# Cross-attention and MoE kernel: fp32 hidden chunks and fp32 w2 in the down product, with no halves of either

## The reference

```python
x = x + xattn(layernorm(x), ctx, w_q, w_kv, w_out, b_out)   # 16 heads of 64, softmax over 77 keys
x = x + ffn(layernorm(x), router_w, w1, w2, w3, sw1, sw2, sw3)

# ffn, x2 = 8192 rows of 128; 8 experts of 176 hidden units; the 2 best experts of a row
logits = x2 @ router_w.T
gate = zeros(T, 8); gate[row, idx of its top 2] += logits
for e in range(8):
    h = silu(x2 @ w1[e].T) * (x2 @ w3[e].T)
    moe_out += gate[:, e:e+1] * (h @ w2[e].T)
sh = silu(x2 @ sw1.T) * (x2 @ sw3.T)                        # the shared expert, all rows
moe_out += sh @ sw2.T
```

## Time and profile before

| | us |
|---|---|
| median of 3 runs | 1155.31 |
| lowest and highest | 1151.79, 1160.76 |
| the profiled execution, its own time | 1144.55 |
| its span, first to last instruction | 1142.7 |
| mean granted TensorE clock | 0.931 |
| PE busy | 956.3 (84%) |
| DVE busy | 900.6 (79%) |
| POOL busy | 736.9 (64%) |
| ACT busy | 716.1 (63%) |

### The profile page before, as it was taken

The page is one execution under the profiler, slowest core; times in us unless marked ns, Lnnn a source line. Parts: engine busy times, 40 slices in busy tenths (PEclk is TensorE's granted clock), DMA queues, the critical chain, the costliest instruction groups (busy, mean ns, idle before and its releaser), DMA issues.

```text
span 1142.7 us, 30302 instructions
## 1 busy us (share of the span) xinstructions
PE 956.3 (84%) x10072; PEld 786.8 (69%) x10072; DVE 900.6 (79%) x2010; ACT 716.1 (63%) x1574; POOL 736.9 (64%) x1141
## 2 busy tenths in 40 slices
PE   5856889999999998889999999887466778888772
PEld 5555778887887876777788787666355667777441
DVE  4676688997997887778799788889436868888994
ACT  3544687777777775556677677654345648777651
POOL 3232467557788777556788787865666646565765
PEclk9879899999999999888999999988678989999996
DMA  8053232533344432222443444434333456566853
GB/s 263 6 180 43 35 61 55 138 61 58 73 74 62 71 71 57 49 49 53 99 73 69 66 72 62 71 76 102 66 93 109 127 142 166 161 165 161 163 143 115
DMA packets 222789, 107.45 MB, mean 94 GB/s; under 512 B 160464, under 2 KB 214384, under 8 KB 221456
## 3 DMA queue, kind: packets, MB, share of 16 engines
q1 hardware_dynamic: 214448, 88.47, 36.3%
q0 software_dynamic: 8192, 17.06, 5.2%
HBM read 39.15 MB, written 35.06 MB: 65 GB/s over the span
## 4 chain that ended last, share of the span: by engine, by line
PE 34%; DVE 18%; issue 15%; POOL 12%; ACT 9%; DMA 9%; SPq 1%; POOLq 0%; DVEq 0%; ACTq 0%
DMA OT_lo<-O_lo 6%; PE Q L1315 5%; PE S L1249 4%; DVE top L1007 3%; POOL O_lo L584 3%; PE W L1204 3%; PE W L1191 3%; DVE pt_lo L1048 2%; PE W L1205 2%; PE W L1206 2%; PE W L1193 2%; PE W L1192 2%; PE S L1302 2%; DVE P L1017 2%; POOL w_raw L609 2%
## 5 line engine op out<-in xcount | busy, mean ns | idle before, releaser
L1048 DVE TENSOR_TENSOR pt_lo<-Q,pt_hi 77x512 f16<-77x512 f32 x256 | 164.9, 680 | 101.0 <-ACT pt_hi L701 100.4
L609 POOL DMA_INDIRECT w_raw<-ys,pos_y x128 | 129.8, 1014 | 73.3 <-issue 37.9
L584 POOL TENSOR_TENSOR O_lo<-O,O_hi 128x512 f16<-128x512 f32 x128 | 147.8, 1175 | 38.2 <-ACT O_hi L709 24.1
L701 ACT ACTIVATE pt_hi<-Q 77x512 f16<-77x512 f32 x256 | 144.8, 590 | 41.5 <-PE Q L1315 40.7
L490 POOL DMA_INDIRECT xs<-x2cat,pos x128 | 133.0, 1039 | 43.0 <-issue 21.8
L1315 PE MATMUL Q<-ident,P 128*77 128x128 f32 x1024 | 155.8, 288 | 1.1 <-ACT P L684 0.7
L1302 PE MATMUL S<-v_hi,pt_hi 96*128 96x65 f16 x1024 | 118.7, 203 | 32.5 <-DVE P L1017 30.6
L1249 PE MATMUL S<-G,xTm 128*128 128x462 f32 (+1 forms) x384 | 144.9, 513 | 0.6 <-ACT G L691 0.6
L1302 PEld LDWEIGHTS S<-v_hi,pt_hi 96*128 96x128 f16 x1024 | 99.3, 101 | 47.5 <-DVE P L1017 38.5
L1315 PEld LDWEIGHTS Q<-ident,P 128*77 128x77 f32 x1024 | 128.9, 156 | 2.6 <-ACT P L684 1.2
L520 POOL TENSOR_TENSOR x2cat<-x2f,x2cat 128x128 f16<-128x128 f32 x64 | 27.3, 427 | 152.3 <-ACT x2cat L666 152.3
(11 more groups left out here) (280 smaller groups left out, 3273.8 us busy)
## 6 DMA issues: line engine op xcount, KB each, us to landing
ys<-ysb SPq DMA_DIRECT2D x44, 256.0 KB
xg_early<-xs SPq DMA_DIRECT2D x60, 132.0 KB
xp<-x2cat SPq DMA_DIRECT2D x64, 64.0 KB, 1.5
y_out<-X SPq DMA_DIRECT2D x16, 256.0 KB
xg_late<-xs SPq DMA_DIRECT2D x28, 132.0 KB
xs<-zero_in SPq DMA_DIRECT2D x3, 1056.0 KB, 10.8
xs<-zero_in SPq DMA_DIRECT2D x24, 132.0 KB, 2.6
X<-x_in SPq DMA_DIRECT2D x1, 2304.0 KB, 9.6
```

The lines of the kernel that those rows point to most:

```text
L584: pool.tensor_tensor(O_lo[:, half_], O[:, (t + 1) % 2, half_], O_hi[:, half_], ALU.subtract).then_inc(s["p_Olo"], 1)
L609: pool.indirect_dma_start(out=Yr[:, q % YR, k, i * D:(i + 1) * D], out_offset=None, in_=ys_d[batch_part(b)][:, :], in_offset=index(pos_y, ...
L701: act.activation(pt_hi[0:NK, j % 2, c * 512:(c + 1) * 512], QB[q_bank(j, c)][0:NK, :], ACT.Copy).then_inc(s["a_PThi"], 1)
L1048: dve.tensor_tensor(pt_lo[0:NK, j % 2, c * 512:(c + 1) * 512], QB[q_bank(j, c)][0:NK, :], pt_hi[0:NK, j % 2, c * 512:(c + 1) * 512], ALU.s ...
```

## The change

h is kept in fp32: DVE writes hC (now with the scale of w3, on all its 48 rows, straight from PSUM rows 64 to 111) and hA into rings of three, and nothing splits them. w2 is one fp32 tensor, scaled once by ACT. `down` is 2 fp32 matmuls per block of 128 rows, 8 per item in the place of 20. `hC_s`, `hA_hi`, `hA_lo`, `high`, `low`, `low_C`, `low_A` and `w2_lo` are gone. All results of routed items leave through ACT. Three orders differ as well: ACT's `O_high` comes before `turn_out` in a slot and no longer after the last `pt_high`; PE's `turn` comes after the ups of an item and no longer before them; `project(65)` comes after `up_B(0)`. `hC` now carries the wait for POOL's zeroing of the ring.

```diff
-        w2_hi = sb("w2_hi", [128, 2 * WE], HF)
-        w2_lo = sb("w2_lo", [128, 2 * WE], HF)
+        w2 = sb("w2", [128, 2 * WE])
...
-        hA_hi = sb("hA_hi", [128, HR, NT], HF)
-        hA_lo = sb("hA_lo", [128, HR, NT], HF)
-        hC_s = sb("hC_s", [128, HR, NT], HF)
+        hA = sb("hA", [128, HR, NT])
+        hC = sb("hC", [128, HR, NT])
...
# POOL
-            pool.memset(hC_s[:, :, :].rearrange("p r n -> p (r n)").bitcast(F), 0.0).then_inc(s["hC_zero"], 1)
+            pool.memset(hC[:, :, :].rearrange("p r n -> p (r n)"), 0.0).then_inc(s["hC_zero"], 1)
-            def low(n):
-                wait(pool, "g_hA", n + 1)
-                wait(pool, "f_y", n - HR + 1)
-                pool.tensor_tensor(hA_lo[:, n % HR, :], hA[:, n % 2, :], hA_hi[:, n % HR, :], ALU.subtract).then_inc(s["p_loA"], 1)
...
# ACT, slot
+                if old:
+                    O_high(0); O_high(1)
                 if any(turns(t)):
                     turn_out(t)
...
                 if now:
                     pt_high(2); pt_high(3)
-                if old:
-                    O_high(0); O_high(1)
...
# ACT, items
-                if on(n - 1, 0, NI):
-                    high(n - 1)
-                if on(n - LAG - 1, 0, NR) and y_on_act(n - LAG - 1):
+                if on(n - LAG - 1, 0, NR):
                     result_out(n - LAG - 1)
...
# DVE
-            dve.scalar_tensor_tensor(w2_lo[:, :], w2_raw[:, :], fs[:, 10:11], w2_hi[:, :], ALU.mult, ALU.subtract).then_inc(s["w2_lo_done"], 1)
...
-                dve.tensor_tensor(hC[0:IC, n % 2, :], WB[1][CG:CG + IC, :], siluC[0:IC, n % 2, :], ALU.mult).then_inc(s["e_hC"], 1)
+                wait(dve, "f_y", n - HR + 1)
+                if n < HR:
+                    dve.wait_ge(s["hC_zero"], 1)
+                dve.scalar_tensor_tensor(hC[0:IC, n % HR, :], WB[1][CG:CG + IC, :], fs[CG:CG + IC, 12:13], siluC[0:IC, n % 2, :],
+                                         ALU.mult, ALU.mult).then_inc(s["e_hC"], 1)
...
-                if on(n - 1, 0, NI):
-                    low_C(n - 1)
-                if on(n - 1, LOW_POOL, NI):
-                    low_A(n - 1)
-                if on(n - LAG - 1, 0, NR) and not y_on_act(n - LAG - 1):
-                    result_out(n - LAG - 1)
...
# PE
-                    pe.matmul(out, hA_hi[:, r, rows], A_hi, start=True, stop=False)
-                    pe.matmul(out, hA_hi[:, r, rows], A_lo, start=False, stop=False)
-                    pe.matmul(out, hA_lo[:, r, rows], A_hi, start=False, stop=False)
-                    pe.matmul(out, hC_s[:, r, rows], C_hi, start=False, stop=False)
-                    last = pe.matmul(out, hC_s[:, r, rows], C_lo, start=False, stop=True)
+                    pe.matmul(out, hA[:, r, rows], w2[:, ds(at, 128)], start=True, stop=False)
+                    last = pe.matmul(out, hC[:, r, rows], w2[:, WE:2 * WE][:, ds(at, 128)], start=False, stop=True)
...
             for n in range(NI + LAG):
-                if any(turns(LAST + n)):
-                    turn(LAST + n)
                 if n + 1 < NR:
                     rows_turn(n + 1)
                 if n < NI:
                     up_C(n, pcs[n])
                     up_A(n, pcs[n])
-                    if n == 0:
-                        project(LAST)
                     up_B(n, pcs[n])
+                if n == 0:
+                    project(LAST)
+                if any(turns(LAST + n)):
+                    turn(LAST + n)
```

More of the change, by code:

```diff
@@ L205, in program @@
                  "d_pick "
[L206 removed]
+                 "f_T e_T f_C f_A f_B f_y e_hC e_hA e_X e_add g_sC g_sA g_y p_gate "
                  "xg0 xg1 xg2 xg3 xg4 xg5 st_y0 st_y1 st_y2").split()
@@ L277, in y_bank @@
             return QB[1] if m > Y_TWO and m % 2 else WB[2]
-        def y_on_act(m):
-            return m % 2 == 0 or m >= LOW_POOL
         def y_out(eng, m):
-            wait(eng, "g_y", sum(y_on_act(i) for i in range(min(m + 1, NR))))
-            wait(eng, "e_y", sum(not y_on_act(i) for i in range(min(m + 1, NR))))
+            wait(eng, "g_y", min(m + 1, NR))
         def rows_of(n):
@@ L538, in x_loaded, with slot @@
                 eng.wait_ge(s[f"ld_x{max(k for k in range(4) if XP[k] <= b)}"], 16)
-            def slot(t, tail=None):
+            def slot(t):
                 if on(t, -1, NB - 1):
@@ L561, in slot @@
                     members(chunk_of(t, S_PLACE))
-                if tail is not None:
-                    tail()
                 if on(t - 4, 0, NB):
@@ L610, in gather @@
                                         in_offset=index(pos_y, b, k)).then_inc(s[f"ga{q % YR}"], 16)
[L612 to L620, removed]
+            for t in range(LAST + 1, TAIL + 1):
+                slot(t)
+            pool.wait_ge(s["w2_done"], 1)
             for q in range(NS):
@@ L762, in slot @@
                     wait(act, "s_G", 4 * NB)
-                    act.activation(w2_hi[:, :], w2_raw[:, :], ACT.Copy, scale=fs[:, 10:11]).then_inc(s["w2_hi_done"], 1)
+                    act.activation(w2[:, :], w2_raw[:, :], ACT.Copy, scale=fs[:, 10:11]).then_inc(s["w2_done"], 1)
             for t in range(FIRST, LAST + 1):
@@ L776, in gate_A @@
                 act.activation(siluA[:, n % 2, :], SB[n % 2][:, :], ACT.Silu, scale=fs[:, 11:12]).then_inc(s["g_sA"], 1)
-            def high(n):
-                wait(act, "f_y", n - HR + 1)
-                wait(act, "e_hC", n + 1)
-                if n < HR:
-                    act.wait_ge(s["hC_zero"], 1)
-                act.activation(hC_s[0:IC, n % HR, :], hC[0:IC, n % 2, :], ACT.Copy, scale=fs[0:IC, 12:13]).then_inc(s["g_hC"], 1)
-                wait(act, "e_hA", n + 1)
-                act.activation(hA_hi[:, n % HR, :], hA[:, n % 2, :], ACT.Copy).then_inc(s["g_hA"], 1)
             def result_out(m):
@@ L1108, in hidden_C @@
                 wait(dve, "g_sC", n + 1)
-                wait(dve, "g_hC", n - 1)
-                wait(dve, "e_loC", n - 1)
-                dve.tensor_tensor(hC[0:IC, n % 2, :], WB[1][CG:CG + IC, :], siluC[0:IC, n % 2, :], ALU.mult).then_inc(s["e_hC"], 1)
+                wait(dve, "f_y", n - HR + 1)
[3 more added lines that the diff above has]
+                                         ALU.mult, ALU.mult).then_inc(s["e_hC"], 1)
             def hidden_A(n):
@@ L1115, in hidden_A @@
                 wait(dve, "g_sA", n + 1)
[L1116 to L1119 removed]
+                wait(dve, "f_y", n - HR + 1)
+                dve.scalar_tensor_tensor(hA[:, n % HR, :], (SB[2], WB[0])[n % 2][:, :], fs[:, 12:13], siluA[:, n % 2, :],
                                          ALU.mult, ALU.mult).then_inc(s["e_hA"], 1)
[L1122 to L1139 removed]
             def X4(q):
@@ L1401, in down @@
                     pe.wait_ge(s["d_res"], NB)
-                    pe.wait_ge(s["w2_lo_done"], 1)
+                    pe.wait_ge(s["w2_done"], 1)
                 if m == Y_TWO + 1:
@@ L1407, in down @@
                 wait(pe, "e_X", before + 1 - NR)
-                for name in ("g_hA", "g_hC", "e_loC"):
+                for name in ("e_hC", "e_hA"):
                     wait(pe, name, m + 1)
-                wait(pe, "p_loA", min(m + 1, LOW_POOL))
-                wait(pe, "e_loA", m + 1 - LOW_POOL)
                 for i in range(GB):
```

29 lines of the change are left out of this document (1 added, 28 removed).

## The result

| | kernel before | changed kernel |
|---|---|---|
| median of the runs, us | 1155.19 (4 runs, 1151.79 to 1160.76) | 1118.04 (4 runs, 1116.58 to 1121.38) |
| profiled execution / its span | 1144.55 / 1142.7 | 1116.58 / 1114.7 |
| ratio of the times | | 0.968, 95% interval 0.963 to 0.972 |

A forecast was written before the change was run, and what follows sets the result against it. PE was taken to bound plain slots, hand-overs the passage, DVE and ACT the items, POOL's gathers the end. Gains of 5 (slots), 8.5 (passage), 7.8 (items) and 4.3 us (end), 25.6 in all, gave 1130 us, range 1112 to 1150.

The forecast's parts named there:

- Down on PE: Down product: 16 fp32 instructions at 0.11 us, 1.76 an item, 0.65 more; items 4.20 routed, 3.75 shared.
- The 0.05 us for hand-overs: Items on PE: 0.05 us added to 4.15 routed and 3.70 shared, giving 4.20 and 3.75.
- Loads not hidden: Rival, down product: 0.19 us per fp32 pass, items 5.5 routed, 5.0 shared, 1180 us as median; chance 0.06.
- The splits: ACT and DVE lose some 1.4 us an item each; only 0.30 routed, 0.34 shared reaches the pace.
- The end: Group 9's first gather to the span's end: 81.2 us instead of 85.5, POOL's rate closing the program.
- The passage: 805 to 940 us: POOL waits give 8.7, item pace 2.8, charges cost 3; item 18 comes 8.5 us earlier.
- The 3 us charged for project(65) and the zeroing: Passage: project(65) ahead of turn(65) waits for OT_lo, and fp32 zeroing delays hC(0); 3 us lost.
- A smaller term: Items 9 to 16: pace from about 4.9 to 4.5 us, 2.8 us gained.
- Taking `low` from POOL: Passage: about 1.2 us an item, mostly beside a scatter on its way, so counted for nothing.
- the passage gives nothing: Rival: scatter landings and project(65) eat the 8.5 us, slots give nothing; 12 us gained, 1143 us; chance 0.17.
- O_high: Slots: 2 us in slots 5 to 9, 3 from OT_lo waits, main part 5 us; plain slots gain nothing.
- The sum: Whole kernel: profiled execution 1144.55 to 1119 us; runs' median, 10.8 above the profiled one, 1155.3 - 25.6, said as 1130.

The follow-up runs named there:

- the four kernels with halves: Profiled kernels whose down product stays in fp16 halves: kernel before (1155.19 us), its repeat (1153.0), PE's new order alone (1150.3), O_high early alone (1135.5).
- the five with fp32: Profiled executions with fp32 down: alone (1130.6 us), with O_high early (1114.4), changed kernel (1118.04), its repeat (1118.5), rows ahead, edges spread, old PE order (1103.0).

## Why the prediction was right or wrong

**Down on PE, right.** 0.11 us an instruction was forecast, 0.112 measured; items of 4.20 and 3.75 were forecast, 4.19 and 3.71 measured (55.6 us from item 44 to item 59). The 0.05 us for hand-overs was not there, ups and down took that much more. "Loads not hidden" fell, with the direct measure of the doubled product behind it. Items 18 to 44: 7.8 us forecast, 8.1 measured.

**The splits, right in the mean.** DVE and ACT lost their 1.4 us an item each, and only what PE did not take was gained. But 4.50 was no item's pace: DVE gave the items without adds 3.8 or 4.3 us, and what there was to gain lay in the items with adds.

**The end, right in kind, too small.** 4.3 us from group 9's first gather to the end was forecast; 1114.7 - 1034.8 = 79.9 against 85.5 makes 5.6. The sentence "shared items being faster than that is worth nothing more" is not borne out: in the 73.5 us from 1034.78 to 1108.25 a step of POOL takes 73.47 / 55 = 1.34 and not 1.36, where the kernel before had 79.06 / 55 = 1.44, and 2.7 us of waits for DVE's adds remain in it. So the end still followed the items' pace.

**The passage, the step that failed.** The term was "the three POOL waits, 11.7 us together, should shrink to about 1 us each", 8.7 us. They are 13.1, and only the third shrank, to 1.12. The reason given was that PE no longer holds an item back and "ACT's gates are done when POOL's data come". PE's ups of item 0 did come about 9 us earlier, but ACT's silu of item 0 did not, since xTm of turn(65) stands ahead of it in ACT's queue. And the prediction did not follow what the turn was moved behind: rows_turn(n+1), so SyncE's load, so SyncE's store, which waits for POOL. Where that ring was opened, the first two waits vanished. The 3 us charged for project(65) and the zeroing were roughly of the right size: hC(0) starts 3.7 us behind siluC(0), where it was 0.1.

The runs show two parts of the passage apart. fp32 with the old PE order gives about 10 us here (153.2 the mean of two, 163.3 the mean of the four kernels with halves), and the new order takes about 6 of them back (159.2, the mean of two). In the medians 1114.4 against 1118.0 and 1118.5 the intervals of the ratios overlap, so the 6 us rest on two profiles of each order. By itself, in the kernel with halves, the order is worth nothing. A smaller term was too low: from item 9 to item 16 the four kernels with halves take 34.7 to 36.5 us and the five with fp32 29.4 to 30.0, about 5 us less, where 2.8 was forecast with a pace of 4.5 us that the forecast's own 4.20 contradicts. Taking `low` from POOL gave little, as forecast, and this is how it shows: POOL's wait for its own scatters to land, at 800 to 930 us, in the kernel before

```profile
POOL x2cat L487 <- DMA xs<-x2cat,pos: 9.6, 11, 1.9
```

and in the changed one:

```profile
POOL x2cat L478 <- DMA xs<-x2cat,pos: 25.6, 12, 2.5
```

16 us more of waiting stand where the splits of hA, some 1.2 us each, lay between the scatters. The rival "the passage gives nothing" named this landing, and for the changed kernel it was nearly true: 1.4 us between the two profiles, 4 between the means of the table.

**O_high, the term that was mis-sized.** "Main: 5 us"; alone it measures 16 (ratio 0.986), and 12 to 15 in the slots of the table. Plain slots gave nothing and the hole took O_hi in, as forecast. The slots of casts that were looked at were not the whole: they gave 2.8 us, and slots 29 to 38, with the first routing tables, gave about 4. The rest is spread over slots in which single executions differ as much. I had bounded only the waits for OT_lo (24.0, now 20.2) and never summed ACT's waits in the slots that are not plain. Which instruction of such a slot turns ACT's earlier O_hi into PE's time is not settled.

**The sum.** 5 + 8.5 + 7.8 + 4.3 = 25.6 forecast; between the two profiles 11.5 to slot 62, 1.4, 8.1 and 7.0 make 28. The further 9 of the 37 come from the kernel before, whose profiled execution was fast for it: I carried its 10.8 us to the changed kernel as well, and this has only 1.5. Two errors in opposite directions, the passage and the slots, nearly cancelled, and the whole came out near the forecast by luck.

## What to carry to other kernels

Before moving an instruction past another on an in-order queue, follow what the other one waits for, through the DMA queue that serves it, back to the engine that is to be freed. In such a ring through SyncE one load more cost about 6 us here; opening it, spreading the clearing DMAs and the old order brought 15 together. Look in every engine's in-order program for what stands ahead of the freed work, too. Where an engine's work is removed between its own DMAs, look for the landing that it hid. Size a change of order from every kind of slot, not from the plain one and one other. A mean pace can be that of no item: list the distances before pricing a change by it.

## What the runs showed of the hardware that was not expected

A small instruction of DVE on one partition can be held for the length of a POOL instruction. Timeline of DVE in the changed kernel, the table step in a slot and the same step, three quarters as wide, in the passage:

```profile
741.39 1.01 DVE L944 TENSOR_TENSOR ctx_raw<-ctx_raw,kc 1x256 f32<-1x256 f32 x1
...
886.25 0.35 DVE L944 TENSOR_TENSOR ctx_raw<-ctx_raw,kc 1x192 f32<-1x192 f32 x1
```

The first starts inside POOL's O_lo and ends 0.28 us behind it, the second stands beside no POOL arithmetic:

```profile
740.42 1.70 POOL L573 TENSOR_TENSOR O_lo<-O,O_hi 128x512 f16<-128x512 f32 x1
```

It is so in all four places of this step in the slots of the two kernels (1.01 or 1.02 us), and 0.35 in both passages. The Trainium skill, page "SBUF — State Buffer", section "Who interferes with whom", says that a DVE instruction with two SBUF inputs contends with a POOL instruction that reads SBUF, and that the pair of ports they share is an exclusive lock; the 1.01 against 0.35 agrees with it, though no run took O_lo away.

PE can be slow for a reason that the profile does not name. On two of the four chips of the experiments the kernel before took 8% longer; whether that belongs to the chip is not shown, since one execution on the first chip took 1242.1 us too. In the kernels that were profiled on those two chips the items pause for 8 to 24 us, first after item 19 (in the kernel with down twice already after item 18), then mostly at the passes in which DVE adds (24, 27, 30 and on). Timeline of ACT on one of them, in the kernel with rows ahead of stores:

```profile
955.08 1.14 ACT L764 ACTIVATE ysb<-Q,xg_late 128x128 f32<-128x128 f32 x4 [18.54 <-remote]
```

The profile names no engine that ends this wait, but PE's own timeline in a later pause shows where the time goes:

```profile
1002.03 0.22 PE L1294 MATMUL Q<-hc,xg_early 128*128 128x128 f16 x1 [0.46 <-issue]
1003.45 0.22 PE L1294 MATMUL Q<-hc,xg_early 128*128 128x128 f16 x1 [1.20 <-issue]
1004.86 0.27 PE L1294 MATMUL Q<-hc,xg_early 128*128 128x128 f16 x1 [1.20 <-issue]
```

PE starts single matmuls 1.4 us apart here that otherwise start 0.056 apart, and waits for nothing that the profile shows. After 935 us this execution has 56 such idle times of PE, over 0.2 us each, and all of them fall within a group of POOL's 8 gathers or at most 4 us behind it. The profiles on the other two chips have none, with the same gathers. What holds PE there stays open.
